# Delta-rule layer: weight preparation divided anew over the first slots, masks first and solved blocks placed by transfers in the steady slots

## The chip, the cores and the metric

One core of one Trainium2 chip runs the whole program in one launch. The metric is the device time of the kernel in microseconds (us), inputs and outputs in the chip's main memory (DRAM below), everything in float32 on the matrix engine except where other layers split into bfloat16. The engines are TensorE (PE), VectorE (DVE), ScalarE (ACT), GpSimd (POOL) and SyncE (SP), which issues transfers (DMAs).

## The reference, cut to what matters

Twelve stages change a residual stream `x` of 16 sequences x 256 tokens x 128 features. The second stage is the one that the diff touches:

```python
x = x + 0.5 * _L0_ffn_ref(_layernorm(x), ...)
x = x + _L0_attn_ref(_layernorm(x), Wq, Wk, Wv, Wbeta, Wo, g_norm)     # this stage
x = x + 0.5 * _L0_ffn_ref(_layernorm(x), ...)
...                                                                     # nine more stages

def _L0_attn_ref(x, Wq, Wk, Wv, Wbeta, Wo, g_norm):     # H = 4 heads, Dk = Dv = 32
    q = _l2norm(split(x @ Wq)); k = _l2norm(split(x @ Wk)); v = split(x @ Wv)
    beta = sigmoid(x @ Wbeta)
    def step(S, (q_t, k_t, v_t, b_t)):                  # scan over 256 tokens
        err = (v_t - k_t @ S) * b_t
        S = S + outer(k_t, err)
        return S, q_t @ S
    o = o * rsqrt(mean(o * o) + 1e-5) * g_norm          # per head
    return o @ Wo
```

## The kernel before, in words

The scan is not run token by token. A sequence has two tiles of 128 tokens. Within a tile the errors of all tokens solve a triangular system (identity plus the strictly upper, beta-weighted Gram matrix of the keys, `a0_A`), one of 128 x 128 for each head. Its inverse is built up: the 32 x 32 diagonal blocks are inverted by substitution on VectorE, then blocks of 64 and 128 are put together by small matmuls (`ax5`, `i21`, `it5`, `x6`, `it6`). Then the errors of the first tile (`err`, c = 0), the state after it (`state`), what is left for the second tile (`rest`), its errors (`err`, c = 1) and the outputs (`o`) follow.

A group `g` is two sequences, that is four tiles of 128 tokens and 16 systems; there are G = 8 groups. The stage is a software pipeline of 12 slots, written out without a loop. `over_slots(parts)` takes for each engine a list of (lag, function), and in slot s it emits, in the order of the list, each function with g = s - lag where that group exists. So the order in the list is the order in which that engine's queue works, in every slot. Lag 0 is the layer norm, lag 1 projections, unit vectors, turning of q, k and beta k, and the key Gram matrix (`agram`), with the products that pick its diagonal blocks (`diag_dve`, L1284); lag 2 is the substitution, lag 3 the query-key Gram matrix (`gram_pe`, L1247), its masks (`mask_dve`, L1274), and all from the blocks to `o`; lag 4 is the output's norm, its turning, the product with Wo and the addition to x (`add_dve`, L1596).

The substitution (L1307 and L1311) works with one of 128 partitions for every half of a diagonal block and goes through rows 30 to 0, each a product and a reduction on VectorE, longer with every row. To get the blocks into this form and back they go through DRAM, issued by `ship_sync` on SP in this order for each group: diagonal out (L1321), solution of the group before out (L1327, two), diagonals in (L1331, two), solution in as blocks (L1336, into `a0_Ic`). VectorE turns these 32 x 32 blocks into `a0_Itc` (`turn_blocks_dve`, L1344), and ScalarE (`spread_act`) copies `a0_Ic` twice into `a0_I02` (L1350), the turned blocks four times into `a0_It` (L1354) and `a0_Ic` twice into `a0_I64` (L1356). `ax5_pe` (L1369) needs `a0_I02` and the key Gram, `i21_pe` needs `a0_It`, `x6_pe` (L1430) needs `a0_I64`.

ScalarE takes four copies of heads into `a0_Z` for each Gram matrix (`heads_act`, L1233): with i = 2 for the key Gram, with i = 0 for the query Gram of the next slot. The latter stands behind `o_act` (L1543) in its list, and `gram_pe` waits for it.

In the gaps of the first slots the stage also prepares the weights of later stages: VectorE quantises (`ffn3_weights_dve`, in slot 1), then, at the end of slot 2, TensorE turns some 33 weight tiles by transposes through two banks (`turns_pe`, L1619), ScalarE copies them out (`turns_act`, L1630), and the functions in `prepare` finish the weights of the single stages (L483 to L492, L614 to L624, L912 to L916, L2400 to L2413) with waits between VectorE, TensorE and GpSimd. At the start GpSimd clears seven buffers (L1681) and ScalarE waits for that.

The list of VectorE before, which the change reorders:

```python
over_slots(
    [(0, with_parity(stats_dve)), (3, mask_dve), (4, square_out_dve), rows(30, 28), (3, turn_blocks_dve),
     rows(27, 23), (1, squares_dve), quantise(0, 2), rows(22, 16), (0, with_parity(apply_dve)),
     (1, unit_dve), (4, norm_out_dve), quantise(2, 3), rows(15, 0), (1, diag_dve), quantise(5, 2),
     (2, at_first(weights_dve)), (4, add_dve)])
```

## Time and profile before

| | us |
|---|---|
| median of 3 runs | 4684.73 |
| lowest and highest | 4678.41, 4695.13 |
| the profiled execution | 4690.88 |
| its span in the trace | 4689.1 |
| mean granted TensorE clock, share of full | 0.915 |

| engine | busy us | share of the span |
|---|---|---|
| TensorE | 4010.2 | 86% |
| VectorE | 3486.6 | 74% |
| ScalarE | 3087.3 | 66% |
| GpSimd | 1514.4 | 32% |

The shares are means over twelve stages with different limits. The stage that the diff touches lies between about 62 and 576 us of the span, which is a ninth of it; what the change is worth is read there. In the rows below the first number is the start in us from the start of the span, the second how long the engine was busy with it, then come engine, line, operation, what is written and read, and shapes. In brackets stands how long the engine had been idle before it, and the instruction that ended the wait. `arena` holds the buffers of the stages, `bank` the matmul results (PSUM).

### The profile page before, as it was taken

The numbers are of one execution on the slowest core, as the hardware profiler recorded it, in microseconds if no ns is written. First come the engines' busy times: TensorE is split into PE (matmuls) and PEld (weight loads), VectorE is DVE, ScalarE is ACT, GpSimd is POOL, SyncE is SP. The second block draws the span as 40 slices with busy tenths as digits, with TensorE's granted clock in tenths as the row PEclk, the third lists the DMA queues.
The fourth block names the chain that finished last, engine by engine and source line by source line (L and its number), as shares of the span: only waits on it lengthen the run. The fifth ranks groups of instructions, "written<-read, shape, count | busy, mean of one in ns | idle before, by whom it ended". The sixth has DMA issues, their size and how long they took to land.

```text
span 4689.1 us, 66058 instructions
## 1 busy us (share of the span) xinstructions
PE 4010.2 (86%) x15980; PEld 2243.5 (48%) x15980; DVE 3486.6 (74%) x11277; ACT 3087.3 (66%) x5681; POOL 1514.4 (32%) x2846
## 2 busy tenths in 40 slices
PE   5688749999999999999999999983977659999965
PEld 3466634444444444444444444432555436676644
DVE  5787569888878888787887887865657945665578
ACT  2455318999989999898998998981222225565532
POOL 2222123444444444444444443433000023333310
PEclk8788679999999999999999999995999779999977
DMA  2111110000000000000000000000000001111100
GB/s 55 23 23 23 24 23 1 1 19 5 8 17 1 20 5 1 22 3 15 10 1 20 5 8 17 1 1 0 0 0 0 0 27 42 37 39 38 40 1 18
DMA packets 132041, 69.78 MB, mean 15 GB/s; under 512 B 92346, under 2 KB 124815, under 8 KB 129317
## 3 DMA queue, kind: packets, MB, share of 16 engines
q1 hardware_dynamic: 124020, 52.62, 4.6%
q10 hardware_dynamic: 7600, 12.58, 0.7%
q8 instruction: 139, 2.28, 0.2%
q14 instruction: 282, 2.30, 0.2%
HBM read 52.39 MB, written 12.80 MB: 14 GB/s over the span
## 4 chain that ended last, share of the span: by engine, by line
PE 54%; DVE 17%; ACT 13%; issue 10%; DMA 3%; POOL 2%; ACTq 1%; DVEq 0%; SPq 0%; POOLq 0%
PE bank L1852 18%; PE bank L1867 6%; PE bank L1896 5%; PE bank L2624 4%; PE bank L1906 3%; DMA packed_dram<-arena 3%; PE bank L647 2%; PE bank L2657 2%; ACT arena L1956 2%; ACT arena L1943 2%; ACT arena L1944 2%; ACT L1990 2%; ACT arena L1947 2%; PE bank L677 1%; DVE xn L326 1%
## 5 line engine op out<-in xcount | busy, mean ns | idle before, releaser
L1852 PE MATMUL bank<-arena 128*128 128x512 f32 x3072 | 1422.7, 596 | 12.8 <-DVE arena L2033 8.1
L1852 PEld LDWEIGHTS bank<-arena 128*128 128x128 f32 x3072 | 586.6, 191 | 756.9 <-issue 727.6
L2093 POOL TENSOR_SCALAR arena<-arena 128x256 f32<-128x256 f32 x1024 | 480.3, 479 | 1188.2 <-DVE arena L2026 1188.2
L1867 PE MATMUL bank<-arena 128*128 128x512 f32 x1024 | 526.0, 605 | 63.9 <-DVE arena L2056 63.6
L2015 DVE SCALAR_TENSOR_TENSOR arena<-arena 128x256 f32<-128x256 f32 x1024 | 393.2, 420 | 195.2 <-ACT arena L1944 188.8
L2056 DVE SCALAR_TENSOR_TENSOR arena<-arena 128x256 f32<-128x256 f32 x1024 | 491.5, 524 | 14.0 <-issue 12.9
L2033 DVE SCALAR_TENSOR_TENSOR arena<-bank,bv,arena 128x256 f32<-128x256 f32 x1024 | 444.7, 472 | 0.0
L1943 ACT ACTIVATE arena<-bank,bqk 128x512 f32<-128x512 f32 x512 | 348.0, 680 | 77.4 <-PE bank L1852 67.7
L2026 DVE SCALAR_TENSOR_TENSOR arena<-bank,bq,arena 128x512 f32<-128x512 f32 x512 | 384.1, 750 | 18.0
L1956 ACT ACTIVATE arena<-arena,const_table 128x512 f32<-128x512 f32 x512 | 374.5, 732 | 0.0
L2635 DVE TENSOR_REDUCE arena<-bank 128x2 f32<-128x512 f32 x256 | 176.2, 688 | 250.5 <-PE bank L2626 250.5
L1947 ACT ACTIVATE arena<-bank,bqk 128x512 f32<-128x512 f32 x512 | 353.8, 691 | 1.1 <-PE bank L1852 1.1
L1944 ACT ACTIVATE arena<-bank,bqk 128x512 f32<-128x512 f32 x512 | 349.3, 682 | 0.0
L1959 ACT ACTIVATE arena<-arena 128x512 f32<-128x512 f32 x512 | 322.6, 630 | 16.3
L2668 ACT ACTIVATE arena<-bank 128x512 f32<-128x512 f32 x256 | 153.3, 599 | 264.1 <-PE bank L2657 210.6
L2611 POOL TENSOR_TENSOR arena<-arena 128x256 f32<-128x256 f32 x256 | 185.9, 726 | 432.8 <-DVE arena L2601 432.3
L2624 PE MATMUL bank<-const_table,arena 128*128 128x256 f32 x1024 | 308.7, 395 | 4.1 <-POOL arena L2611 4.1
L1867 PEld LDWEIGHTS bank<-arena 128*128 128x128 f32 x1024 | 176.8, 190 | 280.6 <-DVE arena L2056 154.8
L1906 PE MATMUL bank<-arena 128*128 128x512 f32 x512 | 264.6, 600 | 0.7 <-ACT arena L1979 0.7
L1896 PE MATMUL bank<-arena 128*128 128x512 f32 x512 | 261.2, 623 | 4.2 <-ACT arena L1986 3.3
L2067 DVE BATCH_NORM_STATS2 arena<-bank 128x6 f32<-128x128 f32 x512 | 113.6, 284 | 200.7 <-PE bank L1923 200.7
L316 POOL TENSOR_SCALAR rstd<-meanvar 128x4 f32<-128x4 f32 x96 | 20.4, 213 | 740.6 <-DVE meanvar L310 690.9
(372 smaller groups left out, 7558.6 us busy)
## 6 DMA issues: line engine op xcount, KB each, us to landing
arena<-packed_dram SPq DMA_DIRECT2D x48, 192.0 KB
arena<-packed_dram ACTq DMA_DIRECT2D x16, 576.0 KB
arena<-diag_dram SPq DMA_DIRECT2D x16, 256.0 KB, 4.0
arena<-in_L_attn_Wk_dram SPq DMA_DIRECT2D x16, 256.0 KB, 3.3
arena<-in_L_attn_Wq_dram SPq DMA_DIRECT2D x16, 256.0 KB, 4.0
arena<-in_L_attn_Wv_dram SPq DMA_DIRECT2D x16, 256.0 KB, 4.5
arena<-in_L_attn_Wo_dram SPq DMA_DIRECT2D x8, 512.0 KB, 3.8
arena<-in_L_attn_W_dram SPq DMA_DIRECT2D x16, 256.0 KB, 2.7
```

The costliest lines, as they stand in the source:

```text
L1852: nc.tensor.matmul(bank[:, RING1[m % 5], :], w1p[k][:, i * P:(i + 1) * P], zT_of(g), start=True, stop=True).then_inc(a1_proj.sem, 1)
L1867: nc.tensor.matmul(bank[:, 6, :], wo1[:, i, :], a1_att[:, i % 4, :], start=(i == 0), stop=(i == NB1 - 1)).then_inc(a1_outd.sem, 1)
L1896: nc.tensor.matmul(bank[:, HBANK[i], :], w1a[:, i * P:(i + 1) * P], a1_x1[:, u, :], start=True, stop=True).then_inc(a1_h_psum.sem, 1)
L1906: one = nc.tensor.matmul(bank[:, 1, :], w1b[:, i, :], a1_h[:, i, :], start=(i == 0), stop=(i == NF1 - 1))
L1943: nc.scalar.activation(a1_ek[:, i % 4, :], k, ACT.Exp, bias=bqk[:, 0, i:i + 1])
L1944: nc.scalar.activation(a1_kf[:, i % 4, :], k, ACT.Relu, bias=bqk[:, 0, i:i + 1])\
L1947: nc.scalar.activation(a1_eq[:, i % 4, :], q, ACT.Exp, bias=bqk[:, 1, i:i + 1])\
L1956: nc.scalar.activation(a1_z[:, i % 4, :], a1_qf[:, i % 4, :], ACT.Ln, bias=table[:, C_TINY:C_TINY + 1]).then_inc(a1_ln.sem, 1)
L2033: last = nc.vector.scalar_tensor_tensor(seqs(a1_ek[:, i % 4, :])[q], seqs(b[2])[q], bv1[:, i:i + 1], seqs(a1_kf[:, i % 4, :])[q], ALU.add, ...
L2056: last = nc.vector.scalar_tensor_tensor(seqs(a1_att[:, i % 4, :])[q], seqs(a1_qf[:, i % 4, :])[q], a1_kv[:, i % 4, q:q + 1], seqs(a1_z[:, ...
L2093: last = nc.gpsimd.tensor_scalar(a, a, 1.0, a1_ksum[:, i % 4, b:b + 1], ALU.add, ALU.mult)
L2624: nc.tensor.matmul(dst, a3_R[:, w % 4, i * P:(i + 1) * P], table[:, C_KEYS:C_KEYS + T], start=True, stop=False)
```

## The change

1. `clear_pool`: the seven clears come behind the first rstd in GpSimd's list; ScalarE waits for them only ahead of the first copy of heads. GpSimd also takes `out_pool` ahead of `unit_pool`.
2. `prepare` gets two new lists. `sums` holds what VectorE can do before the weights are turned, and runs in slot 1. `ended` holds the waits that closed TensorE's functions, and runs behind the last slot.
3. `turns_pe` and `turns_act` go from the end of slot 2 to its front, and use four banks in place of two.
4. Solved blocks: four new transfers on SP write the blocks from DRAM to their places in `a0_I02` and `a0_I64`, each for 32 partitions; ScalarE's four copies (L1350, L1356) go. `ax5_pe` and `x6_pe` wait for the transfers.
5. VectorE's list: masks, three rows, turned blocks, then the squares of the output; the norm and the units later and earlier as shown; `apply_dve` behind `unit_dve`; the products `diag_dve` ahead of the last five rows. The squares of the output use `a0_prod` in place of `a0_Itc`.
6. TensorE's list: `turn_pe` behind `it6_pe`, `agram_pe` behind the first `err_pe`. ScalarE's follows it; the query heads (`heads_act(0, a0_zq)`) come ahead of `o_act`.

```diff
-        prepare = {"tensor": [], "vector": [], "gpsimd": [], "sync": []}
+        prepare = {"tensor": [], "vector": [], "gpsimd": [], "sync": [], "sums": [], "ended": []}
...
-            a0_os = a0_kb
+            a0_os = a0_prod.rearrange("p (q d) -> p q d", q=QT)
...
+            HEAD_ROWS = range(DK0 - 2, DK0 - 5, -1)
...
+                        elif g == 0:
+                            nc.scalar.wait_ge(a0_zeroed, 1)
...
+                        if r == HEAD_ROWS[-1] - 1 and g >= 2:
+                            a0_osq.wait(nc.vector, g - 2)
...
                     if g >= 1:
                         sp.wait_ge(a0_xsent, 32 * g)
+                        rows = v.rearrange("(s p c) -> p s c", p=P, c=DK0)
                         if g >= 2:
-                            a0_spread.wait(sp, g - 2)
-                        sp.dma_start(a0_Ic[:], v.rearrange("(s p c) -> p s c", p=P, c=DK0)).then_inc(a0_xloaded, 16)
+                            a0_p["x5"].wait(sp, g - 2)
+                        for k, at in ((0, 0), (2, 1)):
+                            sp.dma_start(a0_I02[k * DK0:(k + 1) * DK0, :, at * DK0:(at + 1) * DK0],
+                                         rows[k * DK0:(k + 1) * DK0]).then_inc(a0_i02, 16)
+                        if g >= 2:
+                            a0_icd.wait(sp, g - 2)
+                        sp.dma_start(a0_Ic[:], rows).then_inc(a0_xloaded, 16)
+                        if g >= 2:
+                            a0_p["x6"].wait(sp, g - 2)
+                        for k in range(2):
+                            sp.dma_start(a0_I64[k * DK0:(k + 1) * DK0, :, k * DK0:(k + 1) * DK0],
+                                         rows[k * DK0:(k + 1) * DK0]).then_inc(a0_i64, 16)
...
             def spread_act(g):
-                nc.scalar.wait_ge(a0_xloaded, 16 * (g + 1))
-                for k, at in ((0, 0), (2, 1)):
-                    last = nc.scalar.activation(a0_I02[blk(k), :, blk(at)], a0_Ic[blk(k), :, :], ACT.Copy)
-                last.then_inc(a0_spread.sem, 1)
                 a0_icd.wait(nc.scalar, g)
                 for k in range(P // DK0):
-                    nc.scalar.activation(a0_It[blk(k), :, blk(k)], a0_Itc[blk(k), :, :], ACT.Copy)
-                for k in range(2):
-                    last = nc.scalar.activation(a0_I64[blk(k), :, blk(k)], a0_Ic[blk(k), :, :], ACT.Copy)
+                    last = nc.scalar.activation(a0_It[blk(k), :, blk(k)], a0_Itc[blk(k), :, :], ACT.Copy)
                 last.then_inc(a0_spread.sem, 1)
...
-                    a0_spread.wait(nc.tensor, g, 1)
+                    nc.tensor.wait_ge(a0_i02, 32 * (g + 1))
...
+                    nc.tensor.wait_ge(a0_i64, 32 * (g + 1))
...
-                    nc.tensor.transpose(bank[0:cols, 4 + i % 2, 0:rows], src, ident[0:rows, 0:rows])\
+                    nc.tensor.transpose(bank[0:cols, 4 + i % 4, 0:rows], src, ident[0:rows, 0:rows])\
...
+            def sums_dve():
+                for f in prepare["sums"]:
+                    f(nc.vector)
...
-                    [(3, gram_pe), (1, proj_pe)] + both(ax5_pe)
+                    [(3, gram_pe), (1, proj_pe), (2, at_first(turns_pe))] + both(ax5_pe)
                     + [(3, i21_pe(0)), (3, it5_pe(0)), (3, i21_pe(1)), (3, it5_pe(1))]
-                    + both(x6_pe) + [(4, out_turn_pe), (1, turn_pe)] + both(it6_pe) + [(4, out_pe), (1, agram_pe)]
-                    + both(lambda b: err_pe(b, 0)) + both(state_pe)
-                    + both(rest_pe) + [(0, with_parity(transpose_pe))] + both(lambda b: err_pe(b, 1)) + both(o_pe)
-                    + [(2, at_first(turns_pe))])
+                    + both(x6_pe) + [(4, out_turn_pe)] + both(it6_pe) + [(1, turn_pe), (4, out_pe)]
+                    + both(lambda b: err_pe(b, 0)) + [(1, agram_pe)] + both(state_pe)
+                    + both(rest_pe) + [(0, with_parity(transpose_pe))] + both(lambda b: err_pe(b, 1)) + both(o_pe))
+                for f in prepare["ended"]:
+                    f(e)
...
-                e.wait_ge(a0_zeroed, 1)
                 over_slots(
-                    [(1, keep_act), (3, spread_act)] + both(x5_act)
+                    [(1, keep_act), (2, at_first(turns_act)), (3, spread_act)] + both(x5_act)
                     + [(3, i21_act(0)), (3, it5_act(0)), (3, i21_act(1)), (3, it5_act(1))]
-                    + both(x6_act) + [(4, out_act), (1, turn_act), (1, heads_act(2, a0_zk))] + both(it6_act) + [(1, agram_act)]
-                    + both(lambda b: err_act(b, 0)) + both(state_act) + both(rest_act)
-                    + [(0, with_parity(copy_act))] + both(lambda b: err_act(b, 1)) + both(o_act)
-                    + [(2, heads_act(0, a0_zq)), (2, at_first(turns_act))])
+                    + both(x6_act) + [(4, out_act)] + both(it6_act) + [(1, turn_act), (1, heads_act(2, a0_zk))]
+                    + both(lambda b: err_act(b, 0)) + [(1, agram_act)] + both(state_act) + both(rest_act)
+                    + [(0, with_parity(copy_act))] + both(lambda b: err_act(b, 1))
+                    + [(2, heads_act(0, a0_zq))] + both(o_act))
...
-                    [(0, with_parity(stats_dve)), (3, mask_dve), (4, square_out_dve), rows(30, 28), (3, turn_blocks_dve),
-                     rows(27, 23), (1, squares_dve), quantise(0, 2), rows(22, 16), (0, with_parity(apply_dve)),
-                     (1, unit_dve), (4, norm_out_dve), quantise(2, 3), rows(15, 0), (1, diag_dve), quantise(5, 2),
-                     (2, at_first(weights_dve)), (4, add_dve)])
+                    [(0, with_parity(stats_dve)), (3, mask_dve), (2, substitute_dve(HEAD_ROWS)), (3, turn_blocks_dve),
+                     (4, square_out_dve), (1, squares_dve), quantise(0, 2), rows(HEAD_ROWS[-1] - 1, 22), (4, norm_out_dve), rows(21, 15),
+                     (1, unit_dve), (0, with_parity(apply_dve)), rows(14, 5), quantise(2, 3), (1, diag_dve), quantise(5, 2), (1, at_first(sums_dve)), rows(4, 0), (2, at_first(weights_dve)), (4, add_dve)])
...
-                over_slots([(0, with_parity(rstd_pool)), (1, unit_pool), (4, out_pool), (1, values_pool),
+                over_slots([(0, with_parity(rstd_pool)), (0, at_first(clear_pool)), (4, out_pool), (1, unit_pool), (1, values_pool),
                             (2, at_first(weights_pool))])
```

## Rows read from the trace of the kernel before

**Rows 1.** windows of the stage: us, PE, PEld, DVE, ACT, POOL busy (instructions), PEclk, DMA, GB/s
```profile
152.00:171.00 19.00, 10.72 (x25) 4.93 (x25) 6.24 (x25) 3.97 (x16) 3.08 (x11) 0.50 0.39 69
...
278.00:330.00 52.00, 41.15 (x294) 31.27 (x294) 42.44 (x101) 28.33 (x67) 12.09 (x10) 0.84 0.15 26
```

**Rows 2.** timeline, VectorE, steady slot: start, us, instruction [idle before <-releaser]
```profile
274.12 0.69 DVE L1274 TENSOR_TENSOR arena<-bank,const_table 128x512 f32<-128x512 f32 x1 [7.52 <-PE bank L1247]
...
278.55 0.68 DVE L1554 TENSOR_TENSOR arena<-arena 128x512 f32<-128x512 f32 x1
...
282.29 0.70 DVE L1344 STREAM_TRANSPOSE arena<-arena 128x512 f32<-128x512 f32 x1
...
285.83 1.21 DVE L1175 TENSOR_REDUCE arena<-arena 128x32 f32<-128x1024 f32 x1
...
293.57 1.43 DVE L1199 TENSOR_TENSOR arena<-arena 128x256 f32<-128x256 f32 x4
...
295.96 0.69 DVE L1569 TENSOR_TENSOR arena<-arena 128x512 f32<-128x512 f32 x1
...
326.21 0.69 DVE L1274 TENSOR_TENSOR arena<-bank,const_table 128x512 f32<-128x512 f32 x1 [5.44 <-PE bank L1247]
```

**Rows 3.** timeline, VectorE, slot 2: substitution rows 27, 21 and 14, products
```profile
117.67 0.24 DVE L1307 TENSOR_TENSOR arena<-arena 128x80 f32<-128x80 f32 x1
...
122.46 0.34 DVE L1307 TENSOR_TENSOR arena<-arena 128x176 f32<-128x176 f32 x1
...
131.57 0.46 DVE L1307 TENSOR_TENSOR arena<-arena 128x288 f32<-128x288 f32 x1
...
149.68 2.76 DVE L1284 TENSOR_TENSOR arena<-arena,const_table 32x512 f32<-32x512 f32 x4
```

**Rows 4.** timeline of the first slots: GpSimd, VectorE, TensorE, VectorE twice
```profile
62.56 7.44 POOL L1681 MEMSET arena<- 128x2048 f32 x7 [17.88 <-DVE x L440]
...
71.41 1.11 DVE L326 TENSOR_SCALAR xn<-x,meanvar,rstd 128x128 f32<-128x128 f32 x4 [7.29 <-POOL rstd L319]
...
142.48 0.27 PE L1619 MATMUL bank<-const_table,wi 128*128 128x128 f32 x1
...
158.40 0.29 DVE L483 TENSOR_REDUCE w1s<-w 128x1 f32<-128x128 f32 x1 [5.96 <-ACT w3outT L1630]
...
170.95 0.85 DVE L305 BATCH_NORM_STATS2 stats<-x 128x6 f32<-128x128 f32 x4
```

**Rows 5.** timeline, ScalarE, the same steady slot as in 2
```profile
282.35 1.26 ACT L1350 ACTIVATE arena<-arena 32x512 f32<-32x512 f32 x2
```

**Rows 6.** timeline, TensorE, the same slot and the next one's Gram matrix
```profile
296.71 0.93 PE L1578 MATMUL bank<-const_table,arena 128*128 128x128 f32 x4 [3.19 <-DVE arena L1569]
...
303.68 3.80 PE L1258 MATMUL bank<-arena 128*128 128x512 f32 x8 [0.20 <-ACT arena L1233]
...
307.31 1.87 PE L1472 MATMUL bank<-arena 128*128 128x32 f32 x16
...
324.10 5.65 PE L1247 MATMUL bank<-arena 128*128 128x512 f32 x8 [3.04 <-ACT arena L1233]
```

**Rows 7.** timeline, DMA issues of SP at the end of that slot
```profile
321.97 1.11 SPq L1327 DMA_DIRECT2D inverse_dram<-arena  x2
...
324.88 0.36 SPq L1336 DMA_DIRECT2D arena<-inverse_dram  x1
```

**Rows 8.** timeline, VectorE: products of slots 3 and 8, addition right behind T of slot 9
```profile
212.33 2.76 DVE L1284 TENSOR_TENSOR arena<-arena,const_table 32x512 f32<-32x512 f32 x4
...
473.72 2.76 DVE L1284 TENSOR_TENSOR arena<-arena,const_table 32x512 f32<-32x512 f32 x4
...
522.54 0.68 DVE L1596 TENSOR_TENSOR x<-bank,x 128x512 f32<-128x512 f32 x1
```

**Rows 9.** view of DMA issues, whole stage: count, KB each, median us to landing
```profile
inverse_dram<-arena SPq DMA_DIRECT2D x16, 128.0 KB, 2.4
...
arena<-inverse_dram SPq DMA_DIRECT2D x8, 256.0 KB, 4.5
```

60 lines of the change are left out of this document (33 added, 27 removed).

## Prediction, made before the changed kernel ran

> **What bounds the kernel now.** The change touches one stage of twelve, the delta-rule layer, so I read the trace of that stage only, from the stage's start at about 62 us to its last addition at about 576 us, and let the other 4110 us stand. In the windows of that stage VectorE is the busiest engine in every slot, and TensorE's granted clock is not full: 0.84 on the mean of one slot, a mixture of its levels of 1.2 and 2.4 GHz [rows 1]. Next I took VectorE's timeline of one steady slot, from one stage of diagonal products (L1284) to the next. Five steady slots, between the start of that work at 212.33 and at 473.72, take 261.4 us, 52.3 each [rows 8]. The reader is to see one hole in each: VectorE stands still before the first mask (L1274) until TensorE has made the Gram matrix (L1247), 7.52 us in one slot and 5.44 in the next [rows 2]. So a slot is a ring: VectorE's unit vectors (L1199) release TensorE's transposes, these the rest of TensorE's and ScalarE's work, this the Gram matrix, this the masks, and these the next slot's VectorE work. Around the ring TensorE and ScalarE are late, although VectorE is busy some 42 of 52 us. In the first slots there are two other holes: the first normalisation waits 7.29 us, because GpSimd clears seven buffers for 7.44 us ahead of the first rstd, and the weights' preparation at the end of slot 2 holds VectorE for 18.5 us (152.4 to 170.9), of which only 6.24 are work [rows 1, 4].
>
> Below, T is the end of a slot's substitution (the last L1311), "ready" the end of the unit vectors.
>
> **First slots.** (a) `clear_pool` moves behind the first rstd: the 7.29 us wait shrinks to the rstd's own 1.3 or so, a gain of 6.0. The clearing then lies beside the first projections, whose squares need GpSimd only later; nothing else is queued behind it but the second rstd and the first `unit_pool`, neither late. (b) In slot 1 the units come before `apply_dve` (four operations, 1.11): ready(0) comes another 1.1 us earlier, so about 7.1 in all. But the diagonal products wait for TensorE's and ScalarE's chain behind ready, and that keeps its length. VectorE has the same quantising beside it, so its hole there grows back to at most 3 us smaller than the sum; what is left at the start of the products is 7.0. (c) The `sums` functions come ahead into slot 1: one reduction of 0.29 [rows 4] and a dozen small operations; I take 2.7 us, with 2 and 4 as bounds, since with what remains they must fill the 6.24 busy us. Slot 2 so starts 4.3 us earlier. (d) `turns_pe` and `turns_act` go from the end of slot 2 to its front, where TensorE has nothing until VectorE's units of slot 2. Behind them in TensorE's queue stand the transposes and key Gram of slot 2, needed for the diagonal products. The preparation on TensorE took from 142.5 to 170.9 before [rows 4], much of it waiting for VectorE's sums; with those done, four banks and not two, I put it at 20 us from its release, when the last quantising ends near 107. That is 1 to 1.5 us later than the units; I charge 1.5 to slot 2 (bounds 0 and 9). (e) What is left for VectorE at the slot's end is work: 6.24 - 2.7 = 3.5 us in place of 18.5, a gain of 15.0. The waits that closed these functions on TensorE move behind all slots, where they are long met: nothing. Sum: 4.3 - 1.5 + 15.0 = 17.8. Slot 3 gains 1.1 more by the shorter ring, as it also has its hole. Together **18.9 us**, bounds 11 and 22.
>
> **Steady slots, TensorE's and ScalarE's side.** The removed ScalarE copies (L1350 and L1356, two of each and of one shape, 1.26 us a pair) take 2.5 us from ScalarE's chain [rows 5]; there TensorE had slack, since it waited 3.19 us for VectorE's norm before the transposes of the output [rows 6]. So in steady slots they bring nothing by themselves; in the tail they do. From ready (295.9) to the next Gram matrix (324.1) the ring takes 28.2 us [rows 2, 6]. Three pieces go. First, the transposes of the output (0.93) and the norm that they await (0.7) come earlier in the slot, out of the way: 1.55. Second, the error products (L1472, 1.87) come before the key Gram instead of behind it; they fit while ScalarE still copies heads, for which the key Gram waited anyhow (0.20 behind L1233) [rows 6]. I take 1.2 of the 1.87, since ScalarE copies the Gram after it. Third, the copy of query heads goes ahead of `o_act`, so the 3.04 us of the Gram's wait for it vanish [rows 6]. `it6_pe` ahead of the turning brings nothing, by the same wait for heads. The ring's part becomes 28.2 - 1.55 - 1.2 - 3.04 = 22.4 us. The Gram matrix itself (5.65) and the last mask behind it stay at 6.3.
>
> **Steady slots, VectorE's side.** Behind the turned blocks' start VectorE has: the turn 0.70, the output's squares and their sum 1.4, the reduction of squares 1.21 [rows 2], rows 27 to 22 of the substitution 3.7 (117.67 to 122.46, less the 1.1 us of the reduction in between), the norm 0.7, rows 21 to 15 5.8, the units 2.4. So ready comes 16.0 us after the turn starts. GpSimd's pow for the output runs before that for the units, and both fit under the rows. Then: normalisation 1.1, rows 14 to 0 18.1, products 2.8: T comes 22.0 after ready [rows 2, 3]. A slot is therefore 38.0 us plus the time from T to the turn's start. That start has two conditions. By the ring: the Gram starts at ready + 22.4 = T + 0.4, the masks end at T + 6.7, three rows with their clears take 2.2: T + 8.9 where the clock is good, T + 11.0 where it is not (I add the 2.1 us between the two old holes). By the transfers: the blocks were issued 2.91 us after the write of the solution, landing takes 4.5 [rows 7, 9], so T + 7.4 if the write starts at T, which it can because the diagonal's DMA now lies under rows 4 to 0. Two new transfers go ahead of it in SP's queue: 0.36 us each of issue, and half of the same small pieces on the same 16 DMA engines. No row shows these placed copies: the lower bound is 0 (hidden in the spacing), the upper 2.25 (half of 4.5). I take 1.8, near the upper, because the block load moves as much again on the engines that it shares: T + 9.2. The two behind it (`a0_I64`) cost nothing, they are wanted 10 us later by L1430. SP waits anew for `x5`, `icd` and `x6` of the group before, each done since the middle of the last slot, so what is queued behind (the next diagonal) isn't held. TensorE's L1369 waits for the two pieces ahead, with its whole slot queued behind it; they land at about T + 7, and it comes to them after Gram and projections at T + 10. VectorE's turn waits for the block load, with everything of the slot behind it: that is the term of 9.2. So a slot lasts 38.0 + 9.2 = 47.2 or 38.0 + 11.0 = 49.0; 48.1 on the mean. Four slots of 48.1 and one, without the normalisation, of 47.0 are 239.4, against 261.4: **22.0 us**. The engine's own waits that the shared buffers add (squares now in `a0_prod`) are for VectorE's earlier work: nothing.
>
> The Trainium skill, page DMA: Bandwidth & Descriptors, section Rules for kernel authors, speaks against this part: two transfers to disjoint partition halves serialise on the same engines, and one 128-partition transfer is the better choice; its Specifications ask for 512 B or more per piece. The rows fit in so far as 2,048 pieces of 128 B take 4.5 us to land while 128 KB in large pieces take 2.4 [rows 9]. By that rule the placed copies are no cheaper than the copies of ScalarE that they replace, and the rest of the sum stands; taken strictly, it leads to the slower rival below.
>
> **Slot 9 and the tail.** From the products of slot 8 (end 476.5) to T of slot 9 (522.5) are 46.0 us [rows 8]. New: start of the turn at T + 9.2 to 10, then turn, squares of the output, norm and all rows, 30.6: 40.5 us. Gain **5.5**. In the tail TensorE and ScalarE make one chain and VectorE has nothing: turning the blocks ahead of squaring gives 1.4, and of the 2.5 us of copies the half behind the turn gives 1.3: **2.8**.
>
> **Sum.** 18.9 + 22.0 + 5.5 + 2.8 = 49.2 us. The profiled execution took 4690.9 us (span 4689.1); 4690.9 - 49.2 = 4641.7. The median of the runs shown is 6.2 lower, which gives 4635.5. I say 4636.
>
> **Rivals.**
> 1. The ring gives only the removed 3.04 us: the clock stays low through a tightly packed tail of small products, and the rest is taken up again by waits for ScalarE. Then slots are 49.3: 15 us instead of 22.0 and 3 instead of 5.5: 4645. For it: the hole is 2.1 us longer in every second slot, with the same work. Against: the three pieces are seen as waits. Chance 0.22.
> 2. The preparation collides. If it keeps its old length (28 us) at the front of slot 2, `turn_pe`, and with it diagonal and substitution, come 9 us late instead of 1.5: 4643.5. For it: TensorE works through its queue in order. Against: its old length is waiting. Chance 0.13.
> 3. The slower one: transfers. Copies into 32 partitions may take as long as several full ones. The turn then waits: if each of the two pieces ahead cost 6 us of the engines' time, the blocks land at T + 19.4 or so and a slot takes 57.4. The break-even of a steady slot is T + 14.3; that of the kernel, with the 18.9 us of the first slots set against seven such slots, is T + 16.9, which needs 4.8 us for each of the two pieces. At T + 19.4 the kernel takes 4702. For it: 128-byte pieces and no row of such a copy. Against: the full one lands in 4.5. Chance 0.04.
> 4. The change does little in the ring: a wait that I don't see (ScalarE's order at `out_act`, the norm for GpSimd's pow) holds slots at 52, leaving the first slots' gain: 4664. Chance 0.06.
> 5. Better than forecast: blocks land at T + 7.4 and the clock is up, slots of 46.3: 4625. Chance 0.10.
> Forecast itself: 0.45.
>
> **Range.** About 0.3% (14 us) is what a measurement of this kernel can tell from no change. Forecast and rivals 1, 2 and 5 lie between 4622 and 4650; with the bounds of the first slots (8 down, 3 up) and of the landing (7 slots by 1.8 us, 12.6), I give 4618 to 4656. Faster by over 0.3% (below 4670.7): all but rival 3 and half of rival 4, and something for what isn't listed: 0.91. Within 0.3%: 0.05. Slower: 0.04.
>
> **What would show it.** First normalisation at 65.5 and not 71.4; slot 2's hole at VectorE gone, first mask of slot 3 near 153 to 155; wait before the first mask under 2 us; a new wait before L1344's transpose for the DMA if the transfers bind (right if below 1.5 us, rival 3 if over 5); ready 16 us after the turn; five slots in about 239 us. What makes it wrong: a Gram matrix that still starts 5 us after T, or a wait of the products (L1284) for the key Gram's copies in every slot.

## The result, and where the time went

| | before | changed |
|---|---|---|
| median, us | 4689.93 | 4637.68 |
| lowest and highest, us | 4678.41, 4697.31 | 4633.54, 4647.82 |
| profiled execution, us | 4690.88 | 4633.54 |
| its span, us | 4689.1 | 4631.7 |
| mean granted TensorE clock | 0.915 | 0.925 |

The ratio is 0.9895, 95% interval 0.9878 to 0.9913: some 49 us less. 4636 had been forecast, so the total is right. The steps are not all right: errors of up to 6 us in its parts nearly cancel.

Some lines have new numbers: the Gram matrix is now L1262 (L1247), the masks L1289 (L1274), the products L1299 (L1284), the turn of the blocks L1370 (L1344); the substitution is L1324 and L1328, the copies of heads L1248 (L1233). L1344 in the changed kernel is SP's write of the solution.

I measure the stage from the multiplication by `wog` behind which it begins to the end of its last addition. Single executions of the kernel before lie 19 us apart in the table, and 39 (4662.80 to 4702.00) in the 22 of one later round, so a stage length is the finer measure, if it repeats. To see whether it does, both kernels were profiled once more at the end (runs before_again and same_again, below). The runs were made in rounds on different chips: a ratio compares kernels within one round, but the stage lengths compare profiles across rounds, and no run separates the chip's part in their scatter. Slots 4 to 8 and slot 9 of the changed kernel count from the write of the solution (L1344 there) to the next one, those of before from the end of the products, which in either kernel is where a slot's substitution is over.

| part of the stage, us | before | before again | changed | changed again | gain of the means | forecast |
|---|---|---|---|---|---|---|
| first slots, to slot 3's statistics | 108.5 | 108.2 | 92.8 | 93.0 | 15.4 | 17.8 |
| slot 3 | 44.1 | 44.2 | 46.5 | 46.7 | -2.5 | 1.1 |
| slots 4 to 8 | 261.4 | 257.6 | 232.3 | 234.4 | 26.2 | 22.0 |
| slot 9 | 46.0 | 41.1 | 40.1 | 39.3 | 3.9 | 5.5 |
| tail | 53.1 | 50.9 | 49.2 | 48.9 | 3.0 | 2.8 |
| stage | 513.2 | 501.9 | 460.9 | 462.3 | 45.9 | 49.2 |
| the rest of the span | 4175.9 | 4175.9 | 4170.8 | 4174.4 | 3.3 | 0 |

The windows of the changed stage, one for each of five parts (columns as in [rows 1]):

```profile
112.00:154.60 42.60, 18.91 (x62) 10.36 (x60) 39.81 (x104) 14.47 (x41) 13.01 (x19) 0.66 0.08 15
154.60:201.10 46.50, 38.80 (x280) 28.20 (x280) 39.75 (x98) 25.34 (x62) 12.10 (x18) 0.81 0.18 27
...
293.70:340.90 47.20, 39.28 (x295) 28.90 (x294) 42.21 (x101) 25.84 (x63) 13.24 (x10) 0.90 0.22 34
...
433.40:473.50 40.10, 35.32 (x266) 28.02 (x266) 33.73 (x76) 16.04 (x40) 3.11 (x2) 0.76 0.21 34
473.50:522.60 49.10, 36.04 (x269) 32.57 (x268) 9.16 (x15) 13.74 (x36) 6.20 (x4) 0.67 0.15 34
```

A steady slot holds the same VectorE work as before, 42.21 us against 42.44 in [rows 1], but in 47.2 us and not in 52. The next fence is VectorE in that slot, which answers to [rows 2]: addition, masks, clears with the new wait for the diagonal, turn, norm of the output, units, normalisation, products.

```profile
293.58 0.68 DVE L1617 TENSOR_TENSOR x<-bank,x 128x512 f32<-128x512 f32 x1
...
295.81 1.25 DVE L1289 TENSOR_TENSOR arena<-bank,const_table 128x512 f32<-128x512 f32 x2
297.69 0.69 DVE L1289 TENSOR_TENSOR arena<-bank,const_table 128x512 f32<-128x512 f32 x1 [0.62 <-PE bank L1262]
298.55 0.69 DVE L1289 TENSOR_TENSOR arena<-bank,const_table 128x512 f32<-128x512 f32 x1 [0.17 <-PE bank L1262]
300.55 0.48 DVE L1311 MEMSET arena<- 128x512 f32 x1 [1.31 <-DMA arena<-diag_dram]
...
303.11 0.71 DVE L1370 STREAM_TRANSPOSE arena<-arena 128x512 f32<-128x512 f32 x1 [0.20 <-DMA arena<-inverse_dram]
...
309.83 0.68 DVE L1590 TENSOR_TENSOR arena<-arena 128x512 f32<-128x512 f32 x1
...
317.70 0.90 DVE L1216 TENSOR_TENSOR arena<-arena 128x128 f32<-128x128 f32 x4
318.52 1.11 DVE L326 TENSOR_SCALAR xn<-x,meanvar,rstd 128x128 f32<-128x128 f32 x4
...
330.75 3.12 DVE L1299 TENSOR_TENSOR arena<-arena,const_table 32x512 f32<-32x512 f32 x4
```

No wait stands before the first mask; those of 7.52 and 5.44 us in [rows 2] are gone. TensorE shows why. The Gram matrix starts at 292.43, 1.3 us before T, the slot's end at 293.74. Its second half now waits 0.65 us for VectorE's first masks, and the last two masks 0.62 and 0.17 for that half:

```profile
277.92 3.80 PE L1273 MATMUL bank<-arena 128*128 128x512 f32 x8 [0.50 <-ACT arena L1248]
...
292.43 3.45 PE L1262 MATMUL bank<-arena 128*128 128x512 f32 x4
296.53 1.98 PE L1262 MATMUL bank<-arena 128*128 128x512 f32 x4 [0.65 <-DVE arena L1289]
```

Where VectorE waits in the whole stage, in the view of waits: first the row of before, then rows of the changed kernel (total us, times, longest).

```profile
DVE arena L1274 <- PE bank L1247: 57.0, 32, 8.0
```

```profile
DVE arena L1289 <- PE bank L1262: 13.4, 18, 1.8
...
DVE arena L1188 <- ACT arena L1183: 8.0, 2, 6.7
...
DVE arena L1311 <- DMA arena<-diag_dram: 5.8, 4, 2.6
DVE arena L1370 <- DMA arena<-inverse_dram: 4.5, 3, 3.9
DVE arena L1299 <- ACT arena L1281: 3.3, 3, 2.7
```

57.0 us have become 13.4, and two new waits for transfers cost 10.3 together, 3.9 of them in the tail. The transfers themselves, by SP's queue behind the slot's end (write of the solution, diagonals in, two placed pieces, blocks, two placed pieces) and by the view of DMA issues (KB each, median us to landing), answer to [rows 7, 9]:

```profile
293.74 1.11 SPq L1344 DMA_DIRECT2D inverse_dram<-arena  x2
294.89 1.24 SPq L1348 DMA_DIRECT2D arena<-diag_dram  x2
...
296.63 0.84 SPq L1355 DMA_DIRECT2D arena<-inverse_dram  x2
297.51 0.94 SPq L1359 DMA_DIRECT2D arena<-inverse_dram  x1
298.50 2.34 SPq L1363 DMA_DIRECT2D arena<-inverse_dram  x2
```

```profile
arena<-inverse_dram SPq DMA_DIRECT2D x32, 64.0 KB, 3.6
arena<-inverse_dram SPq DMA_DIRECT2D x8, 256.0 KB, 4.8
```

The load of the blocks (L1359) is issued 3.8 us behind the write, and by the median lands 4.8 later: T + 8.6. In the slot shown it is later: the turn, which waits 0.20 us for it, starts at T + 9.4. Before that comes the wait for the diagonals (L1348): they are issued 1.15 us behind T, as the substitution reads their buffer until T, and VectorE's wait for them ends at T + 6.8 here and at T + 5.9 to 6.5 in the other slots that have it (4, 5 and 8). The clears and three rows behind that wait take 2.4 us. So the turn can start at T + 8.3 to 9.2 at the earliest, wherever the blocks are.

The first slots, which answer to [rows 4]: GpSimd's clears, the first normalisation, the reduction of squares, the first and the last of the preparation on TensorE with what follows it, and slot 3's statistics.

```profile
64.92 7.65 POOL L1704 MEMSET arena<- 128x2048 f32 x7
...
65.00 5.53 DVE L326 TENSOR_SCALAR xn<-x,meanvar,rstd 128x128 f32<-128x128 f32 x4 [1.52 <-POOL rstd L319]
...
78.51 1.22 DVE L1188 TENSOR_REDUCE arena<-arena 128x32 f32<-128x1024 f32 x1 [6.67 <-ACT arena L1183]
...
110.09 0.48 PE L1640 MATMUL bank<-const_table,wi 128*128 128x128 f32 x1 [5.87 <-DVE wd L726]
...
119.32 0.39 PE L2442 MATMUL bank<-w3pos,a_shift 128*16 128x128 f32 x2
128.95 2.98 PE L1226 MATMUL bank<-const_table,arena 128*128 128x128 f32 x12 [9.24 <-DVE arena L1216]
...
154.63 0.85 DVE L305 BATCH_NORM_STATS2 stats<-x 128x6 f32<-128x128 f32 x4
```

The normalisation starts at 65.00 in place of 71.41, and then takes 5.53 us in place of 1.11.

### The profile page after: what moved, and what is told of

The parts are those of the page before. It is cut to its first block, busy times and chain, and to the rows that moved or that the text cites. A ratio compares the mean times of both kernels' runs of the same rounds, so it can differ in the third digit from the quotient of the medians.

```text
span 4631.7 us, 66074 instructions
## 1 busy us (share of the span) xinstructions
PE 3976.3 (86%) x15980; PEld 2217.0 (48%) x15980; DVE 3491.4 (75%) x11277; ACT 3068.7 (66%) x5649; POOL 1524.9 (33%) x2846
## 4 chain that ended last, share of the span: by engine, by line
PE 54%; DVE 20%; ACT 12%; issue 8%; DMA 4%; POOL 1%; ACTq 1%; DVEq 0%; SPq 0%; POOLq 0%
PE bank L1877 18%; PE bank L1892 6%; PE bank L1921 5%; PE bank L2653 4%; DMA packed_dram<-arena 3%; PE bank L1931 3%; DVE arena L1324 2%; PE bank L655 2%; PE bank L2686 2%; DVE arena L1328 2%; ACT arena L1969 2%; ACT arena L1968 2%; ACT L2015 2%; ACT arena L1981 2%; ACT arena L1972 2%
```

## The experiments

The theory: in steady slots the ring through TensorE and ScalarE no longer binds, but VectorE's own chain with its two transfers, and this comes from the order of work around the ring; the early diagonal matters because its transfer would otherwise be next. Rivals: that the single step of the query heads does it all, that the placed blocks do, or that the transfers eat part of the gain. same_again is the changed kernel and before_again the kernel before, unaltered; all others but prep_only are the changed kernel with one edit, late_and_first with two. Only order and placement differ. "Stage" is the length defined above. The five steady slots are 232.3 and 234.4 us in the changed kernel's two profiles.

**prep_only: the first slots alone.** The kernel before, with `sums`, `ended` and the moved turns, the steady slots and the clears as they were.

```diff
 # TensorE, ScalarE, VectorE lists of the kernel before
-[(3, gram_pe), (1, proj_pe)] + both(ax5_pe)
+[(3, gram_pe), (1, proj_pe), (2, at_first(turns_pe))] + both(ax5_pe)
-[(1, keep_act), (3, spread_act)] + both(x5_act)
+[(1, keep_act), (2, at_first(turns_act)), (3, spread_act)] + both(x5_act)
-quantise(5, 2), (2, at_first(weights_dve))
+quantise(5, 2), (1, at_first(sums_dve)), (2, at_first(weights_dve))
```

> The kernel before with one part of the change alone: the sums in slot 1 and the turns of weights at the front of slot 2 through four banks; clears, steady order and block copies as before. My theory: the hole of 18.5 us at the end of slot 2 shrinks to 3.5 us and slot 2 starts 2 to 3 us later for the sums, all later slots keep 52 us, so about 13 us less than the kernel before (4677 by its 4690). Rival, that the ring is what counts and the hole only moves to slot 3's masks: under 5 us less.

Measured: stage 494.9 us, with slot 3's statistics at 156.72, 95.4 us into the stage against 108.5 and 108.2 in the kernel before: 13.0 less. Slots 4 to 8 last 47.6, 52.0, 53.8, 52.3 and 53.9, nearly as before, and VectorE waits 55.3 us for the Gram matrix in all. The time, 4680.1 us with a ratio of 0.999 (0.9972 to 1.0007), holds a gain of at most 13 us. The interval of the ratio takes in both 13 us and nothing, so it is the stage that shows the gain: the preparation gives about 13 us and leaves the steady slots alone, as expected.

**old_ring: the ring's order of before on TensorE and ScalarE, and the output's norm behind the units on VectorE; the rest of the change kept** (masks first, early diagonal, placed blocks).

```diff
-[(4, out_turn_pe)] + both(it6_pe) + [(1, turn_pe), (4, out_pe)]
-+ both(lambda b: err_pe(b, 0)) + [(1, agram_pe)] + both(state_pe)
+[(4, out_turn_pe), (1, turn_pe)] + both(it6_pe) + [(4, out_pe), (1, agram_pe)]
++ both(lambda b: err_pe(b, 0)) + both(state_pe)
...
-+ [(2, heads_act(0, a0_zq))] + both(o_act))
++ both(o_act) + [(2, heads_act(0, a0_zq))])
...
-(4, norm_out_dve), rows(21, 15), (1, unit_dve), (0, with_parity(apply_dve))
+rows(21, 15), (1, unit_dve), (4, norm_out_dve), (0, with_parity(apply_dve))
```

> The changed kernel with all of the ring's order undone (norm behind the units, turning ahead of it6, key Gram ahead of the first errors, query heads behind the outputs), the placed transfers, the diagonals ahead of the last five rows and the blocks ahead of the squares kept. My theory: the ring from the units to the Gram matrix is about 26 to 28 us again in place of 20.8, the Gram starts 4 to 6 us after T, and slots take 50 to 52 us instead of 46.4: the stage takes 20 to 35 us more than 461. Rival, that the block transfers and not the ring made the gain: under 8 us more.

Measured: 4675.44 us, ratio to before 0.9981 (0.9962 to 1.0); stage 496.0. The five slots take 260.4 us, which is the 257.6 to 261.4 of before, and slot 9 takes 48.2. The waits come back, in the view of waits and before one slot's masks:

```profile
DVE arena L1289 <- PE bank L1262: 62.0, 30, 9.9
```

```profile
316.34 0.69 DVE L1289 TENSOR_TENSOR arena<-bank,const_table 128x512 f32<-128x512 f32 x1 [8.27 <-PE bank L1262]
```

So masks first, the early diagonal and the placed blocks together are worth nothing in steady slots while the ring is old: all 26 us hang on the ring's order. The placed blocks as the cause are out.

**heads_late: one of that order's three pieces alone**, the copy of query heads behind `o_act` again.

```diff
-+ [(2, heads_act(0, a0_zq))] + both(o_act))
++ both(o_act) + [(2, heads_act(0, a0_zq))])
```

> The changed kernel with the copy of the query heads behind the copy of the outputs again. My theory: the Gram matrix, which now starts about 1.4 us ahead of the end of the substitution, starts 3.0 us later, at T + 1.6; the masks then end near T + 8 and the turned blocks wait for them and no longer for the DMA: each of six slots 1.5 to 3 us longer, 10 to 18 us in all, 4648 to 4656. Rival, that VectorE's own work covers it: under 3 us more.

Measured: 4635.53 us, ratio 0.989 (0.9858 to 0.9922); stage 465.5. The wait is back in full:

```profile
298.69 2.07 PE L1262 MATMUL bank<-arena 128*128 128x512 f32 x2 [3.04 <-ACT arena L1248]
```

but the slot ends at 298.80, so the Gram matrix is still in time. Slots 4 to 8 take 235.1 us, 1 to 3 more than in the changed kernel, and only slot 9 (43.8, its clock at 0.73, a wait of 5.04 before the masks) pays 4 us. My expectation of 10 to 18 us fell, and its rival (under 3 us) holds for slots 4 to 8: the ring has some 3 us of slack, and one piece of 3.04 fits in it. The three pieces aren't three gains that add; together they bring the ring below VectorE's chain, and what goes further is slack. The other two pieces, and masks first, weren't undone singly.

**diag_late: the diagonal behind rows 4 to 0 again.**

```diff
-quantise(2, 3), (1, diag_dve), quantise(5, 2), (1, at_first(sums_dve)), rows(4, 0),
+quantise(2, 3), rows(4, 0), (1, diag_dve), quantise(5, 2), (1, at_first(sums_dve)),
```

> The changed kernel with the diagonal products behind all rows of the substitution, as before. The diagonal's DMA (3.3 us until it is sent) then stands ahead of the solution's in SP's queue. My theory: the blocks land 14.8 us after the last row in place of 8.6, VectorE waits for them about 4 to 5 us ahead of the turn, and a slot takes 49 to 50 us instead of 46.4: the stage takes 15 to 22 us more than 461. Rival, that the transfer's place is of no matter since VectorE's order is full anyway: under 4 us more.

Measured: 4657.28 us, ratio 0.9941 (0.9923 to 0.996); stage 479.1, 17 to 18 more than changed. The slots are 49.2 to 50.4 us, as expected. The wait is the one for the diagonal's transfer, 24.0 us in all where the changed kernel has 5.8; that for the blocks is 3.8:

```profile
DVE arena L1311 <- DMA arena<-diag_dram: 24.0, 6, 5.3
```

So the second limit lies close behind the first: with the new ring the early diagonal is worth 15 us in slots 4 to 8 (248.6 against 233.4), with the old one nothing. The new ring without it still saves 11 us there (248.6 against 259.5).

**act_copies: blocks placed by ScalarE's copies again, not by transfers.**

```diff
-a0_p["x5"].wait(sp, g - 2)
-for k, at in ((0, 0), (2, 1)):
-    sp.dma_start(a0_I02[...], rows[...]).then_inc(a0_i02, 16)
...
+nc.scalar.wait_ge(a0_xloaded, 16 * (g + 1))
+for k, at in ((0, 0), (2, 1)):
+    last = nc.scalar.activation(a0_I02[blk(k), :, blk(at)], a0_Ic[blk(k), :, :], ACT.Copy)
+last.then_inc(a0_spread.sem, 1)
```

> The changed kernel with ScalarE's four copies again in place of the four placed transfers. Read by the stage's own length in the trace (461 us in the changed kernel, from the preparation of wog to the last addition), since runs scatter by some 10 us. My theory: in steady slots VectorE binds and the ring has over 2.4 us to spare, as the late heads showed, so the 2.5 us of copies cost under 0.5 us a slot; the block load lands 1 us earlier after T; the tail is up to 1.3 us longer: 461 to 465. Rival, that the copies stand in the ring: 2.5 us in each of seven slots, 475 and more.

Measured: 4641.34 us, ratio 0.99 (0.9856 to 0.9944); stage 462.2, slots 4 to 8 232.9: the changed kernel's numbers. The sixteen placed pieces of a kind are worth at most a microsecond or so. That was expected: ScalarE isn't late there.

**block_first and four_ahead: the order of the loads in SP's queue.** In block_first the blocks' load goes ahead of the two placed pieces; in four_ahead all four pieces go ahead of it.

```diff
 # block_first
-for k, at in ((0, 0), (2, 1)):
-    sp.dma_start(a0_I02[...], rows[...]).then_inc(a0_i02, 16)
 sp.dma_start(a0_Ic[:], rows).then_inc(a0_xloaded, 16)
+for k, at in ((0, 0), (2, 1)):
+    sp.dma_start(a0_I02[...], rows[...]).then_inc(a0_i02, 16)
```

```diff
 # four_ahead
+for k in range(2):
+    sp.dma_start(a0_I64[...], rows[...]).then_inc(a0_i64, 16)
 sp.dma_start(a0_Ic[:], rows).then_inc(a0_xloaded, 16)
-for k in range(2):
-    sp.dma_start(a0_I64[...], rows[...]).then_inc(a0_i64, 16)
```

> The changed kernel with the block load for VectorE's turn issued ahead of the two pieces for a0_I02. My theory: the two pieces ahead cost the block load their issue (0.9 us) and little more; the turn comes 1 us earlier where it waited for the DMA (3.9 us in slot 10, 0.9 in two others), so the tail is 1 us shorter and the slots alike: 459 to 461 for the stage. Rival, the prediction's 1.8 us for their share of the DMA engines on top of the issue: 2.5 us in the tail and 1 us in some slots, 455 to 458.

> The two pieces of the sixth squaring go ahead of the blocks' load too: four placed pieces ahead instead of two. This sizes a piece ahead. By the prediction's 0.9 us for each piece the load lands 1.8 us later and VectorE's turn waits for it: slots 47 to 48.5, stage 468 to 473. By the trace of the changed kernel (issue of the load 3.8 us behind the write with two pieces ahead, landing 4.8, as with none) only the issue counts, some 0.9 to 1.0 us for the two, of which the turn's slack takes part: slots 46.3 to 47.3, stage 461 to 467. Slower rival (a piece costs 3 us or more of the shared engines): load at the write + 15, slots above 50, stage above 480.

Measured: block_first 4637.04 us, ratio 0.9921 (0.9894 to 0.9949), stage 452.9, slots 4 to 8 231.0. four_ahead 4645.31 us in one execution, stage 461.1, slots 4 to 8 234.7. Between no piece ahead and four there lie 3.7 us in five slots, 0.2 for each piece and slot, with a scatter of 2 us in such a sum. By SP's queue the load is issued 2.9, 3.8 and 4.9 us behind the write with none, two and four pieces ahead, and lands 4.9, 4.8 and 4.5 later (medians). So a piece costs its issue, some 0.5 us, and nothing of the engines' time that these rows could show. Most of that doesn't reach the slot, since the diagonals keep the turn from starting earlier: in block_first no wait for the blocks is left, and the one for the diagonals is 8.8 us instead of 5.8. The slower rival of the prediction needed 4.8 us a piece.

Block_first's stage fell below what either expectation allowed (455 at least), but not mostly for its edit. Of its 8.0 us against the first profile of the changed kernel 6.7 lie in the tail (42.5 against 49.2). There TensorE's clock differed; windows from 10 to 30 us behind the end of slot 9, first block_first, then the changed kernel:

```profile
483.70:493.70 10.00, 8.72 (x141) 8.16 (x141) 0.69 (x1) 7.26 (x17) 2.81 (x1) 1.00 0.18 63
493.70:503.70 10.00, 9.52 (x78) 8.94 (x77) 0.69 (x1) 3.68 (x16) 0.00 (x0) 0.96 0.01 2
```

```profile
483.50:493.50 10.00, 8.29 (x107) 7.65 (x107) 0.69 (x1) 6.23 (x15) 3.10 (x2) 0.68 0.17 63
493.50:503.50 10.00, 9.51 (x80) 8.87 (x78) 0.69 (x1) 4.48 (x16) 0.00 (x0) 0.84 0.01 2
```

The last sixteen error products (L1493) took 1.87 us in the one and 3.46 in the other. Whether the edit had moved the clock or chance had was open, and late_and_first answers it below.

**clear_first and clear_late: where the clears stand.** First ahead of the first rstd, as in the kernel before; then behind the second.

```diff
 # clear_first
-[(0, with_parity(rstd_pool)), (0, at_first(clear_pool)), (4, out_pool)
+[(0, at_first(clear_pool)), (0, with_parity(rstd_pool)), (4, out_pool)
 # clear_late
-[(0, with_parity(rstd_pool)), (0, at_first(clear_pool)), (4, out_pool)
+[(0, with_parity(rstd_pool)), (1, at_first(clear_pool)), (4, out_pool)
```

> The changed kernel with GpSimd's seven clears ahead of the first rstd again, all else as changed. In the changed kernel's trace the first normalisation starts 6 us earlier, but its four operations take 5.53 us instead of 1.11 beside the clears. Theory of the slowed neighbour: the normalisation takes 1.1 us again and starts at about 70.7, so slot 2 starts only 1 to 1.5 us later and the kernel takes about 4639. Rival, the prediction's own term: 6 us later, 4644.

> The changed kernel with the clears one slot later, behind the second rstd. Theory of the slowed neighbour: the first normalisation starts at 65.0 and takes 1.1 us, the squares' reduction comes about 4.4 us earlier (74.1 instead of 78.5), and what is left of it at the start of slot 2 is 2 to 4 us: about 4634. Rival, that the 5.53 us has another cause than the clears: it stays 5.5 us and the time 4638.

Measured: clear_first 4647.06 us, ratio 0.9917 (0.9891 to 0.9943), stage 461.6. The median is nearer to the rival's 4644 than to 4639, but the stage is the changed kernel's (460.9 and 462.3), and slot 2 starts 1 us later, as the theory had it. So the move that the prediction valued at 6 us isn't to be seen in the stage at all. clear_late 4634.5 us, ratio 0.9885 (0.9851 to 0.9918), stage 455.5. The normalisation, in clear_late:

```profile
65.98 1.11 DVE L326 TENSOR_SCALAR xn<-x,meanvar,rstd 128x128 f32<-128x128 f32 x4 [1.51 <-POOL rstd L319]
...
69.84 7.36 POOL L1704 MEMSET arena<- 128x2048 f32 x7
74.82 1.22 DVE L1188 TENSOR_REDUCE arena<-arena 128x32 f32<-128x1024 f32 x1 [6.41 <-ACT arena L1183]
```

It takes 1.11 us when no clear runs beside it. The reduction of squares starts 12.1 us into the stage, against 16.7 in the changed kernel and 17.9 in clear_first. The clears aren't quite free in their new place either: GpSimd's next operation starts at 77.18, though the reduction that it needs ended at 76.04.

**late_and_first, same_again, before_again: both edits, and the scatter.**

```diff
 # late_and_first
-[(0, with_parity(rstd_pool)), (0, at_first(clear_pool)), (4, out_pool)
+[(0, with_parity(rstd_pool)), (1, at_first(clear_pool)), (4, out_pool)
...
-for k, at in ((0, 0), (2, 1)):
-    sp.dma_start(a0_I02[...], rows[...]).then_inc(a0_i02, 16)
 sp.dma_start(a0_Ic[:], rows).then_inc(a0_xloaded, 16)
+for k, at in ((0, 0), (2, 1)):
+    sp.dma_start(a0_I02[...], rows[...]).then_inc(a0_i02, 16)
```

> Both edits that made the stage shorter in one profile each: the clears behind the second rstd (stage 455.5 instead of 460.9) and the solved blocks' load ahead of the two placed pieces (452.9). If both gains are the edits' own they add: 447 to 448, and a kernel time of 4621 to 4625 from the profiled 4633.5. Rival: 6.3 of the 8.0 us of the load's edit were TensorE's granted clock in the tail, which follows what ran before it; then the sum is 453 to 456 with a tail of 49 us, and the time stays within 4628 to 4640, not to be told from the changed kernel.

> The changed kernel once more, nothing altered. The readings of the other runs rest on the length of the stage in one profiled execution each, so this says how well that length repeats. Theory 1 (the differences between the stages of the variants come from their edits): the stage takes 460.9 us within 1.5, the slots 46 to 47 each, and in the tail (480 to 500 us) TensorE's granted clock is again near 0.5 for 10 us, the tail 49 us. Rival (the clock in the tail falls where it will, from execution to execution): the slots repeat, but the tail may take 43 us, and the stage then 455. Time 4634 to 4648.

> The kernel before once more, nothing altered, for its profile: the gain of the stage (513.2 us before, 460.9 and 462.3 in two profiles of the changed kernel) leans on one profile of before. If its waits are those of the order of its work, the stage takes 511 to 515 us again, five steady slots 259 to 264, with a wait of 5 to 8 us before each first mask. If the profiled execution of before was an unlucky one of the clock, the stage takes 507 or less, and up to 6 us of the measured gain are scatter. Time 4680 to 4700.

Measured: late_and_first 4635.69 us, ratio 0.9886 (0.9861 to 0.991), stage 453.8; same_again 4640.98 us, ratio 0.9895 (0.9872 to 0.9919), stage 462.3; before_again 4679.58 us in one execution, stage 501.9. The tail of late_and_first takes 48.6 us, as the changed kernel's 49.2 and 48.9 do: the 6 us of block_first's tail weren't its edit's. The gain at the clears stays: slot 3 ends 135.8 us into the stage, and 135.1 in clear_late, against 139.3 and 139.7 in the changed kernel, about 4 us. Slots 4 to 8 take 230.5, some 2 to 4 less, as in block_first. The rival held: the gains don't add to 447. The stage is 7 to 8.5 us shorter than the changed kernel's, which the times (5.3 us apart, with overlapping intervals) neither show nor deny.

same_again has a slot that shows what the new order still hangs on. From 248 to 298 us it takes 49.5 us and not 46.4. Its windows over 20 us of that slot, and the key Gram with the products that wait for its copy:

```profile
268.00:288.00 20.00, 17.01 (x84) 12.56 (x83) 16.56 (x39) 9.80 (x19) 0.28 (x1) 0.66 0.00 1
```

```profile
280.83 6.30 PE L1273 MATMUL bank<-arena 128*128 128x512 f32 x8
...
287.79 2.77 DVE L1299 TENSOR_TENSOR arena<-arena,const_table 32x512 f32<-32x512 f32 x4 [2.54 <-ACT arena L1281]
```

In the first profile the same window has a clock of 0.91 and the key Gram 3.80 us. The clock, a mixture of the levels of 1.2 and 2.4 GHz, so reaches the time through the key Gram's copy, which the products wait for.

before_again corrects the baseline, as its rival had it (507 or less). With nothing altered, its stage is 11.3 us shorter than the first profile's, while the rest of the span is the same 4175.9. Its first-mask waits stand in two groups; two neighbouring slots:

```profile
273.98 0.69 DVE L1274 TENSOR_TENSOR arena<-bank,const_table 128x512 f32<-128x512 f32 x1 [8.55 <-PE bank L1247]
...
323.61 0.69 DVE L1274 TENSOR_TENSOR arena<-bank,const_table 128x512 f32<-128x512 f32 x1 [3.40 <-PE bank L1247]
```

With a short wait a slot takes 49 to 50 us, with a long one 54 to 55. From ready to the Gram matrix TensorE needs 31.2 us in the one (240.6 to 271.9) and 25.9 in the other (295.6 to 321.5); the prediction had one reading, 28.2, from between (its own profile has 25.0 to 30.4). 3.04 of each is the wait for the heads, as in [rows 6].

## Why the prediction was right or wrong

**Total: right, by luck in part.** Forecast gain 49.2 us, by the median ratio 49. By the means of two profiles each the first slots give 6.0 us less than forecast, slots 4 to 8 4.2 more, slot 9 1.6 less; the stage gives 45.9, and the rest of the span 3.3, of which nothing was forecast. That rest, 4170.8 and 4174.4 us in the changed kernel, is up to 4187 in its variants, which leave that part alone: scatter. In one pair of profiles the stage's gain is 52.3, in the crossed pair 39.6. Terms to a tenth of a microsecond from one execution were false precision.

**First slots, 18.9 forecast (17.8 and 1.1), 12.9 measured (15.4 and -2.5).** Step (a) failed. The first normalisation did start at 65.0 (65.5 forecast), but the sentence "the 7.29 us wait shrinks to the rstd's own 1.3 or so, a gain of 6.0" took VectorE's work beside the clears at its old duration. It took 5.53 us, and 4.4 of the 6.0 were given back at once. Of its four instructions the first two lasted 4.43 and 4.23 us, begun 0.3 us apart, the others 1.05 and 0.86; alone one takes 0.34. The squares' reduction starts only 1.2 us earlier into the stage, and the unit vectors are ready 2.2 us earlier, of which (b) gives its 1.1 as forecast; (a) and (b) had promised 7.1. The sums took 2.0 us (2.7 forecast). Slot 2 started 50.3 and 50.5 us into the stage instead of 51.4 and 51.3: 1 us earlier, where (a) to (c) had promised 4.3. Of the 15.4 us of the first slots prep_only has 13.0; clears and the order of the units give the other 2.4. The prediction named the cover of the clears and looked only at what is queued behind them on GpSimd, not at who works beside them. The Trainium skill, page SBUF — State Buffer, section SBUF: two separate sides, says that VectorE in a two-port mode and GpSimd share one port pair under an exclusive lock: whoever starts first has it for the whole instruction, and the other blocks. The trace agrees as to the kind (1.11 alone, 5.53 beside the clears), though no row shows that this normalisation runs in such a mode. But the hold lasts longer than one instruction of GpSimd's: the longest of the seven clears takes 1.81 us. The first two normalisations end at 69.43 and 69.50, just behind the third clear's end at 69.35, the last two at 70.47 and 70.53, just behind the fourth's at 70.39. So VectorE was held through three clears that followed each other without a gap.

Step (d), the turns' collision, was charged at 1.5 us: VectorE has no wait in slot 2, which is 0.6 us longer than before (39.2 against 38.6). The preparation on TensorE runs from 110.1 to 119.7, 10 us and not 20, and TensorE then stands idle for 9.24 us until VectorE has the units. Rival 2 is thereby out. Step (e) was right: what VectorE has left at the end of slot 2 is 3.3 us (3.5 forecast), a gain of 15.2 (15.0). For slot 3 I forecast a gain because it "also has its hole"; it lost 2.5. The first row is VectorE's in the kernel before, the others in the changed one:

```profile
173.19 0.69 DVE L1274 TENSOR_TENSOR arena<-bank,const_table 128x512 f32<-128x512 f32 x1 [0.85 <-PE bank L1247]
```

```profile
158.75 0.69 DVE L1289 TENSOR_TENSOR arena<-bank,const_table 128x512 f32<-128x512 f32 x1 [1.57 <-PE bank L1262]
...
165.47 1.22 DVE L1188 TENSOR_REDUCE arena<-arena 128x32 f32<-128x1024 f32 x1 [1.29 <-ACT arena L1183]
```

That hole was small: all masks of slot 3 waited 2.1 us in the kernel before, and wait 2.6 now. New are 1.3 us for ScalarE before the sum of squares and 0.3 before the products. VectorE's busy time in the slot is the same (39.6 and 39.7 us).

**Steady slots, 22.0 forecast, 26.2 measured.** The direction and the mechanism were right: no steady slot has a wait before its first mask (slot 9 has one of 1.78), ready comes 15.5 us after the turn's start (16.0), T comes 22.1 after ready on the mean (22.0). The five slots were to take 239.4 us and took 232.3 and 234.4, 46.5 and 46.9 each: the length of rival 5's slots (46.3), though the blocks land at T + 8.6 and not at its T + 7.4. The mis-sized term is the start of the turn: T + 10.1 on the mean of the slots was forecast, as half of them were to have the Gram matrix 2.1 us late; it is T + 8.6 to 9.5, 9.0 on the mean. The ring takes 20.9 us from ready to the Gram matrix in the slot shown and 19.3 in the next (22.4 forecast), so the clock's swings are mostly taken up by slack. It is shorter than the three pieces make it, and a higher clock of TensorE goes with that, for which the prediction had no term: in slots 4 to 8 TensorE was busy for 210.3 and 208.0 us before at a granted clock of 0.81 and 0.82, for 193.6 and 194.4 after the change at 0.87 and 0.88, and in old_ring for 212.8 at 0.78. The clock was higher with the new order each time, but no run separates what the clock gives and what the order. The opening reading, that VectorE is the busiest engine in every slot, held for the window shown, but in slots 5, 7, 8 and 9 of the same profile TensorE was busier (slot 7, from 370.5 to 424.4 us: 43.02 against 42.05). The changed kernel's slots last 45.2 to 47.2 us apart from the one of 49.5, those of before 49.1 to 54.8: the change removes the ring's wait and most of its scatter together. That the removed waits were read as additive was wrong, as heads_late shows. Rival 4, slots that stay at 52 us, is out, and rival 1, in which only the 3.04 us count, too: given back alone they cost 0.7 to 2.8 us in five slots, not 15, and 4 in slot 9.

**The transfers.** Landing at T + 9.2 was forecast, T + 8.6 measured (median); the two pieces ahead were put at 1.8 us, and by block_first (T + 7.8) they cost 0.9, their issue. The bounds were 0 and 2.25, and I took a value near the upper without a row that asked for it. The rule of the Trainium skill (page DMA: Bandwidth & Descriptors, section Rules for kernel authors) against transfers to partition halves, on which the slower rival leaned, fits in so far as a placed piece of 64 KB lands in 3.6 us and the 256 KB load in 4.8; the pieces are no bargain, but they run beside that load, and going against the rule costs nothing measurable in the slots (act_copies). What the prediction missed is that the diagonals' transfer, not the blocks', is waited for first (L1311, 5.8 us, and 24.0 in diag_late). It had written "it can because the diagonal's DMA now lies under rows 4 to 0". That is so of the way out to DRAM alone. The way back (L1348) still starts 1.15 us behind T, and with the masks done by T + 5.5, as in the slot shown, it is what the three rows ahead of the turn wait for; the sum had no term for it.

**Slot 9 and the tail.** 5.5 forecast; 3.9 by the means, from 1.0 to 6.7 by the pairs, because slot 9 of before took 46.0 in one profile and 41.1 in the other. The tail's 2.8 stand against 3.0, while its length can differ by 6 us with the clock (42.5 against 48.6 in block_first and late_and_first, which have the same tail). In that part neither term is settled by two profiles. That the placed copies bring their 1.3 us in the tail wasn't seen: act_copies' tail takes 49.5 us, the changed kernel's 49.2 and 48.9.

**Left open.** Why the clock in the tail was higher in some runs: of the changed kernel and its variants block_first has 42.5 us at 0.78, heads_late and four_ahead 46.2 and 46.6 at 0.72, all others 48.6 to 49.5 at 0.67 or 0.68 (old_ring 0.71). Why the clears held two normalisations through three of them. And how much of the ring's gain is the clock's.

## What to carry to other kernels

Where two engines wait for each other around a ring, removing waits pays only until the ring is shorter than the work of the other engine; count the slack that is left, not the sum of the waits removed, and look which transfer is next (here the early diagonal was worth nothing without the new ring, and the new ring 11 us without it and 26 with it). When work is moved "under" another engine's, ask what the two share: GpSimd's clears beside VectorE's normalisation gave back 4.4 of 6.0 us. Profile the kernel before twice, because a loop that waits on a TensorE whose clock moves can differ by 11 us in a stage with nothing changed.
